# Selectors of the adjacency builder made one half ahead on VectorE, and an edge table laid in one pass, in a seven-layer graph kernel

## The reference

```python
# relational layer (0, 1, 2 of the first block; 4 and 5 of the third):
#   agg[dst] += h[src] @ W[etype];  h = relu(agg + h @ loopw + bias) (+ residual)
# mean layer (3, edge weighted; 6, unweighted):
#   agg[dst] += x[src] * weight;  deg[dst] += weight
#   x + concat([x, agg / max(deg, 1)]) @ W.T + b
# a layer norm over the features follows layers 2, 3, 5 and 6
```

## Time and profile before

| | us |
|---|---|
| median of three runs | 7132.64 |
| the three runs | 7103.35 to 7148.30 |
| the profiled execution's own time | 7121.17 |
| its span, first to last instruction | 7118.9 |
| mean granted TensorE clock in it | 0.808 |

### The profile page before, as it was taken

One profiled execution on the slowest core, in us unless ns is written; L12 is line 12 of the kernel. 1 busy time (PEld: TensorE's weight loads), 2 busy tenths in 40 slices (PEclk: granted clock), 3 DMA queues, 4 the chain that ended last, 5 costly groups with the idle time before them and its releaser, 6 DMA issues.

```text
span 7118.9 us, 132757 instructions
## 1 busy us (share of the span) xinstructions
PE 5280.1 (74%) x25722; PEld 4285.0 (60%) x25723; DVE 3967.8 (56%) x10739; ACT 1620.4 (23%) x3108; POOL 3900.0 (55%) x4125
## 2 busy tenths in 40 slices
PE   6766667777777777777899866666676676667998
PEld 4655666666666666666555466665656666655554
DVE  3222226666666666666666555555545555556665
ACT  1111113322323222222100122222232222221000
POOL 6777776666666666666200066666656666662000
PEclk8777778988989889888899967767666666677998
DMA  3222224444444444444688544444434444445886
GB/s 97 63 67 67 70 69 115 125 124 121 128 123 115 120 114 123 117 117 116 198 285 279 192 118 121 123 120 125 121 110 117 114 119 114 113 117 192 277 284 201
DMA packets 719129, 966.83 MB, mean 136 GB/s; under 512 B 103155, under 2 KB 601199, under 8 KB 718543
## 3 DMA queue, kind: packets, MB, share of 16 engines
q0 software_dynamic: 131872, 271.19, 16.1%
q10 hardware_dynamic: 481717, 354.21, 15.9%
q1 hardware_dynamic: 105210, 338.21, 14.2%
HBM read 608.12 MB, written 361.06 MB: 136 GB/s over the span
## 4 chain that ended last, share of the span: by engine, by line
PE 52%; issue 15%; DVE 13%; POOL 9%; DVEq 6%; ACT 2%; DMA 1%; ACTq 0%; POOLq 0%; SPq 0%
PE msg L1067 17%; PE agg L946 10%; POOL bulk L630 9%; PE sum L1056 8%; DVE acc L1296 8%; PE sum L972 8%; PE msg L972 6%; DVEq L1296 2%; ACT bulk L763 2%; DVE bulk L1381 1%; DVE bulk L1386 1%; PE lin L920 1%; DMA bulk<-in_x_dram,srcT_i 1%; DVEq L159 1%; DVEq L1377 1%
## 5 line engine op out<-in xcount | busy, mean ns | idle before, releaser
L630 POOL DMA_INDIRECT bulk<-h_table,srcT_i x3276 | 3107.7, 949 | 2272.3 <-issue 927.8
L946 PE MATMUL agg<-bulk 128*128 128x196 f32 (+1 forms) x4992 | 1228.2, 364 | 1129.4 <-DVE bulk L1386 572.0
L1296 DVE TENSOR_TENSOR acc<-msg,acc 128x16 f32 x4160 | 728.9, 175 | 2307.5 <-PE msg L1067 1811.4
L1056 PE MATMUL sum<-bulk 128*128 128x128 f32 x8320 | 1539.2, 337 | 345.4 <-DMA bulk<-in_x_dram,srcT_i 210.0
L1056 PEld LDWEIGHTS sum<-bulk 128*128 128x128 f32 x8320 | 1383.2, 244 | 463.9 <-issue 251.2
L946 PEld LDWEIGHTS agg<-bulk 128*128 128x128 f32 (+1 forms) x4992 | 812.7, 188 | 1243.5 <-issue 1201.6
L733 ACT ACTIVATE bulk<-agg 128x392 f32<-128x392 f32 x1664 | 826.5, 497 | 2462.1 <-PE agg L946 2411.2
L1377 DVE TENSOR_TENSOR bulk<-iota_ps,low_key 128x392 f32<-128x392 f32 (+1 forms) x1664 | 927.9, 558 | 277.1 <-issue 277.1
L763 ACT ACTIVATE bulk<-sum 128x512 f32<-128x512 f32 x1040 | 621.1, 597 | 1680.3 <-PE sum L1056 1602.7
L630 POOL DMA_INDIRECT bulk<-in_x_dram,srcT_i x819 | 777.5, 949 | 279.5 <-issue 257.8
L1067 PE MATMUL msg<-bulk,mix_w 128*128 128x128 f32 x4992 | 834.3, 326 | 112.2 <-ACT bulk L763 101.2
(11 more groups left out here) (170 smaller groups left out, 1014.9 us busy)
## 6 DMA issues: line engine op xcount, KB each, us to landing
adjacency_w<-bulk ACTq DMA_DIRECT2D x416, 392.0 KB
adjacency_n<-bulk ACTq DMA_DIRECT2D x416, 392.0 KB
bulk<-adjacency_w SPq DMA_DIRECT2D x147, 896.0 KB, 4.6
bulk<-adjacency_n SPq DMA_DIRECT2D x147, 896.0 KB, 5.0
lent<-h_table SPq DMA_DIRECT2D x6656, 0.5 KB
bulk<-h_table,srcT_i POOLq DMA_INDIRECT x3276
lent<-in_x_dram SPq DMA_DIRECT2D x1664, 0.5 KB
bulk<-adjacency_w SPq DMA_DIRECT2D x49, 448.0 KB, 4.2
```

Of the source, the lines that this page charges most:

```text
L630: nc.gpsimd.indirect_dma_start(out=rows_in[:, s, :], out_offset=None, in_=rows_of[:, :], in_offset=bass.IndirectOffsetOnAxis(ap=srcT_i[:, ...
L946: last = nc.tensor.matmul(AGG[:, w * LOWS:(w + 1) * LOWS], row[:, w, :], of[:, w, :], start=True, stop=True)
L1056: last = nc.tensor.matmul(SUM[q % 2][:, t * KEYS:(t + 1) * KEYS], rows_in[:, 4 * q + t, :], onehot[:, 4 * q + t, :], start=True, stop=True)
L1296: nc.vector.tensor_tensor(acc[:, at], MSG[h][:, s * WIN:(s + 1) * WIN], acc[:, at], ALU.add).then_inc(added, 1)
```

## The change

`hots` and `fill_at` take the list of fills to make (`some`). In the layers with fills, VectorE makes the selectors of fills 0 and 1 of a half before the `adds` of the half in front of it, and those of fills 2 and 3 where all four were made. For the first half of a layer's last pass fills 0 and 1 are made in `opened`, before its wait on `acc_set`. Apart from that, SyncE's pass in layer 0 is split: the passes before the last lay no part of the edge table, the last one does, and GpSimd's wait on `edges_out` is on a constant; one `apart` (a count of waits passed) behind it goes. The diff:

```diff
@@ lend_passes (sync)
-                with sp.Fori(0, P) as p:
+
+                def lend_pass(p, laying):
                     K = sp.snap(P * (REL_BEFORE[l] * QUADS) + p * QUADS)
                     for n in range(QUADS):
                         fetch(l, n, sp.snap(K + n))
                         place(n, sp.snap(K + n))
-                        if l == 0:
+                        if laying:
                             table_part(n)
+
+                if l:
+                    with sp.Fori(0, P) as p:
+                        lend_pass(p, False)
+                    return
+                more = sp.value_load(passes[0:1, 1:2], min_val=0, max_val=MAX_PASSES - 1)
+                with sp.If(more > 0):
+                    with sp.Fori(0, more) as p:
+                        lend_pass(p, False)
+                lend_pass(more, True)
@@ gpsimd
                 if l == 0:
                     pool.wait_ge(at_set, 1)
-                    pool.wait_ge(edges_out, pool.snap(P * (16 * (3 * QUADS - WEIGHTS_FROM)) + 32))
-                    apart(pool)
+                    pool.wait_ge(edges_out, 16 * (3 * QUADS - WEIGHTS_FROM) + 32)
                     gather_lists()
@@ vector
-                def hots(H, at, weighted):
-
-                    for f in range(4):
+                def hots(H, at, weighted, some=range(4)):
+
+                    for f in some:
                         dve.wait_ge(filled, H * 4 + (f + 1))
...
-                    def fill_at(i, h):
+                    def fill_at(i, h, some):
+
                         of, part_of = layer["fills"]
                         at = dve.snap(i * 2 + (part_of * 2 * TURNS + h))
-                        hots(dve.snap(at + (more_slices + 1) * HALVES) if of else at, at, of == 0)
+                        hots(dve.snap(at + (more_slices + 1) * HALVES) if of else at, at, of == 0, some)
 
                     def opened(p):
 
                         onehots(0, 0, dve.snap(count(P, p, r, 0)))
+                        if layer["fills"] and p is more:
+                            fill_at(0, 0, (0, 1))
                         dve.wait_ge(acc_set, 2 + CHUNKS * (r + 1))
 
                     def turn(i, k, filling=False):
                         if filling:
-                            fill_at(i, 0)
+                            fill_at(i, 0, (2, 3))
                         onehots(1, i, k)
+                        if filling:
+                            fill_at(i, 1, (0, 1))
                         adds(0, i, k)
                         if filling:
-                            fill_at(i, 1)
+                            fill_at(i, 1, (2, 3))
                         with dve.If(i < TURNS - 1):
-                            onehots(0, nc.s_assert_within(i + 1, min_val=1, max_val=TURNS - 1,
-                                                          skip_runtime_bounds_check_because="the condition above"), k + 1)
+                            following = nc.s_assert_within(i + 1, min_val=1, max_val=TURNS - 1,
+                                                           skip_runtime_bounds_check_because="the condition above")
+                            onehots(0, following, k + 1)
+                            if filling:
+                                fill_at(following, 0, (0, 1))
                         adds(1, i, k)
```

## The result

The changed kernel takes 6490.97 us, the median of four runs (6484.63 to 6494.16), against 7140.47 of the kernel before beside it (four runs, 7103.35 to 7152.13). The ratio is 0.9098, with a 95% interval from 0.9068 to 0.9128. The profiled execution took 6494.16 us with a span of 6492.1, where the one before took 7121.17 with 7118.9. The mean granted clock went from 0.808 to 0.862. The forecast was 6540, with a range from 6450 to 6720.

The account below looks back on a forecast made before the run. It took GpSimd's gathers to bound layer 0, and TensorE's repeated wait for VectorE's selectors to hold the layers with fills. Terms: 7121.2 - 641.3 (GpSimd's wait) + 80 (kept) - 20 (layer ends) = 6540 us; range 6450 to 6720.

Parts of the forecast that it names:

- layer ends: At the ends of four layers TensorE follows the last gather directly: 5 us each, 20 in all (0 to 25).
- The stall before fill 0: TensorE's 2.7 us wait for VectorE's selectors in each half goes: 1129 us off TensorE, under 150 left.
- The cap: In the layers with fills, gathers become the limit, so the gain is at most GpSimd's 641.3 us wait for sums.
- The floor: GpSimd's gathers set at least 1010 us for each layer with fills, 9.7 us for each of 104 halves.
- chunk steps and starts: GpSimd waiting kept in layers 1, 2, 4 and 5 for steps and layer starts: 80 us, between 0 and 160.
- VectorE's addition: One more selector call per half costs VectorE 0.7 us (0.2 to 1.3), giving 9.5 us per weighted half.
- the first rival: VectorE takes over in layers 1 and 2 at 10.1 us a weighted half: 6620 us in all, chance 0.18.
- The new wait: VectorE stands at `filled` for fill 1, adds queued behind; 1.1 us for selectors, covered by a 1.4 us margin.
- VectorE in front: In layers 1 and 2 VectorE becomes the limit, 40 us over 1010 in each: 6620 us, chance 0.18.
- the moved stall: TensorE's stall moves to fill 2 and half of GpSimd's wait stays: 6860 us, chance 0.11.
- The slower clock: TensorE's pauses for landings keep layers 1 and 2 at 1.2 GHz: 7563 us in all, chance 0.03.
- A shared port: VectorE's selectors hold up gathers, 36 us in each of two layers: 6612 us, chance 0.02.

Follow-up runs that it names:

- table_only: Only the split SyncE pass and GpSimd's constant wait, selectors in the old order, against the changed kernel; 7146.27 us, ratio 1.001.
- after_six: Changed kernel with a quarter of the gathers left out (slots 0, 4, 8 and 12 gathered in a layer's first turn only); 5647.07 us, ratio 0.7926.
- three_ahead: Changed kernel with the selectors of fills 0, 1 and 2 made ahead, instead of 0 and 1; 6485.64 us.
- before_six: Kernel before with slots 0, 4, 8 and 12 gathered in a layer's first turn only; 8134.8 us, where the unedited kernel before took 9163.13.

## Why the prediction was right

The mechanism held in each step; the time was 46 us below the forecast (6494.2 profiled against 6540), inside the range. By its own terms:

| term | forecast | measured |
|---|---|---|
| GpSimd's wait for sums goes, less what is kept | -641.3 + 80 = -561 | -568.5 |
| layer ends and all else between the gathers | -20 | -57.3 |
| opening selectors, SyncE, GpSimd | 0 | not apart; table_only +-0 |
| layer 0 | 0 | -1.0 |

**The stall before fill 0** was forecast to go, and 25.9 of 1129.1 us are left, under the 150 named. **The cap** was forecast from GpSimd's wait: of 1129 us of stall, 626.8 reached the end. That the limit behind it is the gathers' was argued then and is shown now by the pair with an eighth of them gone.

**The floor and what is kept: two errors that cancel.** The floor was put at 1010 us a layer and 80 us were added for chunk steps and starts. The layers came out at 1024.5 to 1032.1, but not because of these steps. A wait in this view runs from the end of one gather to the start of the next, and 0.30 us of that is the gap that stands there without any wait, where the profile calls it issue. The 641.3 us came in 62 + 65 + 73 + 82 = 282 waits in the four layers, so 85 of them were gap that stays; the issue share of the group duly grew from 927.8 to 967.4, and the 34.8 us that still bear TensorE's name stand in 102 waits of 0.34 us, hardly more than the gap. The floor is 819 x 1.25 = 1024 us, and the steps keep next to nothing: the slack, forecast at 5.4 us a half, was enough. The failed steps are "(1041.4 - 21.7) / 819" and "Without that wait layer 1 is 1013.4 us", both of which subtract whole waits, and the term of 80 us, whose true size is about 4 (34.8 less 102 gaps). With the gathers' own 1.4 us less, the group closes the account of these layers: -606.5 + 39.6 - 1.4 = -568.3.

**Layer ends** are the term that was mis-sized: 20 forecast, 25 as its upper end, 57.3 measured (10.2 from layer 1 to 2, 15.2 from 2 to 4 with layer 3 in it, 10.9 from 4 to 5, 21.3 behind layer 5, less 0.3 lost between 0 and 1). Of the last, 6.2 us lie in mean layer 6 itself, which was forecast unchanged to 5 us. The forecast took one stall and "some backlog" off; the timelines of the end of layer 1 show how much backlog it was. The kernel before:

```profile
2253.14 0.60 PE L1104 MATMUL lin<-ident,y 128*128 128x128 f32 x4
2262.00 0.95 POOL L630 DMA_INDIRECT bulk<-h_table,srcT_i  x1 [27.14 <-DMA h_table<-rows]
```

The changed one:

```profile
2116.27 0.94 POOL L641 DMA_INDIRECT bulk<-h_table,srcT_i  x1 [0.30 <-issue]
2125.19 0.60 PE L1114 MATMUL lin<-ident,y 128*128 128x128 f32 x4
2134.15 0.98 POOL L641 DMA_INDIRECT bulk<-h_table,srcT_i  x1 [16.94 <-DMA h_table<-rows]
```

The last product of the layer's linear step starts 18.3 us after the last gather's end before (2234.9 to 2253.14) and 8.0 after (2117.2 to 2125.19). TensorE used to be 10.3 us further behind GpSimd than now, a whole half, where the forecast took 5; from there to the next layer's first gather it is 8.9 and 9.0 us. My reading is that a loop held by TensorE runs its row slots full, so GpSimd is ahead by what they allow. The slots hold two halves, and one of them shows as backlog here. No run changed their number.

**VectorE's addition** was put at 0.7 us a half, between 0.2 and 1.3. It is nothing. Layer 1 less its waits for messages and fills is 1032.1 - 101.1 - 34.0 = 897.0 us, 8.6 a half, where it was 8.8 before; layer 2 is 8.8, where it was 8.9; and after_six, less the same two waits, gives 8.3 and 8.7. The extra call's register work was counted as added time, but the gaps that the profile calls issue before these selectors shrank in layer 1 from 57.9 us in 103 to 26.0 in 43. That the queue now does this work while a selector or a wait is still running is my reading, and no run tried it alone. With that the first rival loses its price, and the forecast wait for messages of some 50 us a layer came out at 101.1 and 78.5.

**The new wait** for `filled` ended nothing: it is there (34.0, 29.8, 7.8 and 16.2 us by layer), behind it the adds came in time, and the margin at fill 2, forecast at 1.4 us, was 4.1 in the timeline above, for TensorE now also waits for rows before it gets there. three_ahead multiplied the wait to 455 us, at no cost.

**The rivals.** VectorE in front, and the moved stall, are out by the numbers above: no layer is over 1050 us with VectorE free of waits, and TensorE waits for selectors for 25.9 us in all. Both come back in after_six, where the gathers no longer set the pace. The slower clock is out: 0.92 in layers 1 and 2 with pauses for landings in them, and 0.81 and 0.80 in layers 4 and 5 where it was 0.70 and 0.68. TensorE is busy for 851 us of the window of layer 1 as before, but the window is 1050 us and no longer 1182, so its idle time fell from 331 to 199 us. That agrees with the Trainium skill's tie of the clock to how busy the array is (TensorE: Matmul & The Clock Gate, Part 1), though no run here varies it by itself. A shared port does not show either: with VectorE busy for 766 of 1050 us instead of 773 of 1182 the gathers last 941 at least and 947 in the median, as before. The prediction asked more of the Trainium skill's rule than it states (SBUF — State Buffer, "Who interferes with whom"): a tensor_scalar takes the shared port pair only where its operands meet the conditions of a two-port mode. These selectors read their source from PSUM (`iota_ps` in the earlier trace rows), and no run shows the mode they ran in, so the unchanged gathers neither bear out that rule nor speak against it.

## What to carry to other kernels

When an engine's stall is taken away, what reaches the end is set by the next limit, and the other engine's own wait measures how far below it stands: 1129 us of stall were worth 627 here. Take the usual gap between two instructions off each wait before you call it recoverable, and add the backlog that the slow engine carries into each phase's end (10.3 us here, one of the two halves that its buffers hold). To tell whether an engine holds a loop, thin out its work and leave the rest: if nothing moves, it does not.

## What was not expected of the hardware

- Idle time that a trace puts down to a releaser includes the gap that would be there anyway: 0.30 us at each gather, 85 of the 641 us here.
- One call more in each half, with its register work, did not lengthen VectorE's time outside its waits: 8.8 and 8.9 us a half in layers 1 and 2 before, 8.6 and 8.8 after, 8.3 and 8.7 in after_six.
- With a quarter of the gathers gone TensorE was granted 0.99 and 0.97 in layers 1 and 2, against 0.92 in the changed kernel and 0.89 and 0.87 in the kernel before.
- On two chips the same program took 9163.13 and 8982.54 us instead of 7130. In the five kernels traced there the gathers kept their 945 ns, and what was longer were register instructions (53 ns to as much as 721, in before_six) and waits whose releaser is not in the program. What it was, these runs don't show.
